# GpSimd scales by the reciprocal sum with "multiply, add zero" in place of "multiply"

## The reference

```python
x = x + ternary_linear(moe(x, cond))                 # layer 0: 8 experts, 2 chosen, 2 shared
c = attention(x)                                     # layer 1: 16 heads of 64, one null key
x = x + quantised_ffn(c)

def attention(x, attn_bias, mask, ...):
    xn = layernorm(x, g_in)
    q = heads(xn @ Wq) * scale; k, v = xn @ Wkv      # one key and value head for all 16 query heads
    sim = q @ k.T + attn_bias                        # (batch, 16, 512, 513 with the null key)
    sim = where(causal or not mask, -max, sim)
    attn = softmax(sim)
    return layernorm(attn @ v @ Wo, g_out)
```

## Time and profile before

| what | value |
|---|---|
| median of 3 runs | 1531.45 us (1531.21 to 1536.43) |
| the profiled execution: its time | 1530.96 us |
| the profiled execution: span of its instructions | 1528.9 us |
| busy PE / DVE / ACT / POOL | 1307.4 / 1059.4 / 762.5 / 870.0 us |
| instructions of POOL | 834, of which 512 are `normalise` (L837) |
| mean granted clock of TensorE | 0.933 of full speed |

### The profile page before, as it was taken

How to read it: one execution, slowest core, us unless ns; L and a number is a source line. 1 busy time by engine, 2 the same in 40 slices (tenths; PEclk the granted TensorE clock), 3 DMA queues, 4 the chain that set the end, 5 groups by cost and what they waited for, 6 DMA issues and landing times. The chain is left out here.

```text
span 1528.9 us, 30048 instructions
## 1 busy us (share of the span) xinstructions
PE 1307.4 (86%) x8710; PEld 1008.9 (66%) x8710; DVE 1059.4 (69%) x2788; ACT 762.5 (50%) x1940; POOL 870.0 (57%) x834
## 2 busy tenths in 40 slices
PE   4979999999934788999999999999999999963865
PEld 3868787778822566777777777777777777751222
DVE  5576666665564665887886777777878867862986
ACT  3313222223212444666665666666666666633853
POOL 1343332323323999778777777787787788930004
PEclk8999999999966788999999999999999999986987
DMA  6222210222026000001001000000000000202215
GB/s 219 101 81 98 97 65 32 96 83 74 10 76 220 15 1 1 1 2 30 2 2 31 1 24 7 2 29 3 2 29 2 2 16 1 72 1 59 69 42 178
DMA packets 51043, 71.55 MB, mean 47 GB/s; under 512 B 4497, under 2 KB 43665, under 8 KB 48850
## 3 DMA queue, kind: packets, MB, share of 16 engines
q1 hardware_dynamic: 50338, 69.60, 13.6%
q10 hardware_dynamic: 560, 0.20, 0.1%
HBM read 57.07 MB, written 12.72 MB: 46 GB/s over the span
## 5 line engine op out<-in xcount | busy, mean ns | idle before, releaser
L837 POOL TENSOR_SCALAR scores<-scores,att_rinv 128x128 f32<-128x128 f32 (+3 forms) x512 | 546.3, 1081 | 67.4 <-DVE att_rinv L1049 67.4
L893 ACT ACTIVATE scores<-scores,att_top 128x128 f32<-128x128 f32 (+3 forms) x512 | 282.9, 553 | 298.4 <-DVE att_top L1031 298.2
L1031 DVE CUSTOM_DVE_ANT_0 scores<-ps_y,w_bias_b,null_s 128x128 f32<-128x128 f32 x448 | 230.2, 548 | 131.9 <-PE ps_y L1181 118.7
L261 POOL TENSOR_TENSOR act_w<-act_g,wide_w 128x512 f32<-128x512 f32 x64 | 105.6, 1650 | 279.5 <-DVE act_g L379 273.9
L1180 PE MATMUL ps_y<-k_hh,q_hl 128*128 128x256 f32 (+2 forms) x512 | 191.0, 383 | 31.3 <-issue 17.8
L1192 PE MATMUL ps_up<-ident,scores 128*128 128x128 f32 x1280 | 192.5, 279 | 25.5 <-ACT keep L901 22.5
L1202 PE MATMUL ps_a<-keep,w_val 128*64 128x128 f32 x2560 | 201.6, 288 | 0.3 <-DVE keep L1059 0.3
L1192 PEld LDWEIGHTS ps_up<-ident,scores 128*128 128x128 f32 x1280 | 153.6, 142 | 51.8 <-issue 24.2
L208 ACT ACTIVATE hid_hi<-hid 128x512 fp32r<-128x512 f32 x80 | 50.5, 632 | 252.7 <-DVE hid L397 250.5
L1202 PEld LDWEIGHTS ps_a<-keep,w_val 128*64 128x64 f32 x2560 | 138.8, 139 | 42.7 <-issue 36.8
L1181 PE MATMUL ps_y<-w_k_lm,w_q_hm 128*128 128x256 f32 (+2 forms) x512 | 165.7, 333 | 0.0
(11 more groups left out here) (236 smaller groups left out, 2648.9 us busy)
## 6 DMA issues: line engine op xcount, KB each, us to landing
wide_w<-token_w_dram SPq DMA_DIRECT2D x16, 1024.0 KB, 4.7
x_raw<-in_x_t_dram SPq DMA_DIRECT2D x8, 512.0 KB, 3.8
x_nat<-in_x_nat_dram SPq DMA_DIRECT2D x8, 512.0 KB, 4.6
x_dram<-x_nat SPq DMA_DIRECT2D x8, 512.0 KB, 2.9
w_x1t<-x_dram SPq DMA_DIRECT2D x8, 512.0 KB, 4.0
c_dram<-out_raw SPq DMA_DIRECT2D x8, 512.0 KB, 3.3
c2t<-c_dram SPq DMA_DIRECT2D x8, 512.0 KB, 3.7
x_tile<-x_dram SPq DMA_DIRECT2D x8, 512.0 KB, 4.4
```

Source lines behind the costliest of these rows:

```text
L261: nc.gpsimd.tensor_tensor(act_w[:, k % 2], act_g[:, k % 2], wide_w[:, k], ALU.mult).then_inc(sem.act_w_ready, 1)
L837: nc.gpsimd.tensor_scalar(s, s, rinv[:, pp, q, hh:hh + 1], None, ALU.mult).then_inc(sem.p_normed, 1)
L893: nc.scalar.activation(s, s, ACT.Exp, scale=-1.0, bias=top[:, pp, q, hh:hh + 1], accum_out=lsum[:, pp, q, hh:hh + 1]).then_inc(sem.exp_don ...
L1031: dve.tensor_tensor_reduce(scores_of(pp, hh, q), psS[:, hh, 0:n], bias_of(w, h)[:, CAUSAL[q]:CAUSAL[q] + n], 1.0, null_s[:, par, q, h:h + ...
```

## The change

GpSimd's `tensor_scalar` in two places gets a second operation. The result is the same number (adding 0.0). No instruction is added, removed or moved on any engine: each engine's stream has the same rows in the same order as before. The first place runs 16 times (128 x 1280, the factor is the constant -1.0), the second 512 times (the four widths, the factor is a value for each partition read from `att_rinv`).

```diff
@@ def mask_diagonal(pool, nc, w, h, sem):
     pool.wait_ge(sem.bias_in[h], 16 * QB)
-    nc.gpsimd.tensor_scalar(bias_of(w, h), bias_of(w, h), -1.0, None, ALU.mult).then_inc(sem.bias_turned, 1)
+    nc.gpsimd.tensor_scalar(bias_of(w, h), bias_of(w, h), -1.0, 0.0, ALU.mult, ALU.add).then_inc(sem.bias_turned, 1)
     pool.wait_ge(sem.bias_turned, h + 1)
@@ def normalise(J, j):
                         s = scores_of(pp, hh, q)
-                        nc.gpsimd.tensor_scalar(s, s, rinv[:, pp, q, hh:hh + 1], None, ALU.mult
+                        nc.gpsimd.tensor_scalar(s, s, rinv[:, pp, q, hh:hh + 1], 0.0, ALU.mult, ALU.add
                                                 ).then_inc(sem.p_normed, 1)
```

## The result

The changed kernel takes 1494.6 us (median of 4, 1493.01 to 1495.32) beside 1532.72 us of the kernel before in the same runs: a ratio of 0.9744, 95% interval 0.9726 to 0.9763. The forecast was 1486 in a range of 1466 to 1504. The gain is 38 us, where the terms of the forecast add up to 45.

A forecast was written before the change was run, and what follows sets the result against it. TensorE was taken to bound the steady batches and GpSimd batch 0 while it has bias to turn. Terms of -25, -8, -6, -2 and -4 sum to -45 us on 1530.96: 1486 us, range 1466 to 1504.

The forecast's parts named there:

- Batch 0 is bound by GpSimd: Batch 0 from 522.9 us: TensorE becomes the bound, the stretch goes from 105.2 to about 80 us, -25 us.
- The 79.7 us that the steady pace gave: Batch 0 from 522.9 us: its 49 runs of L837 at the pace of 64 in a 104.1 us steady batch.
- The price: Multiply-add on GpSimd: 0.83 ns an element, 293 to 612 ns for the scores' four widths, 1250 ns for the bias.
- Start of batch 0: 482.8 to 522.9 us: 5 us back from VectorE's holds, 3 from earlier turns and quicker matmuls, -8 us.
- Steady batches: Six batches and the last: TensorE stays the bound, its idle time shrinks by 1 us a batch, -6 us.
- The mixture: Second batch, with the two early heads of bias: shorter VectorE holds leave about 1 us of the loss, -4 us.
- End of attention: Last eight score multiplications after the last reciprocal take 3.6 us instead of 8.50, -2 us.
- Rival 1: Scores and bias: only the constant-factor form is quick; 1501 us, chance 0.07.
- rival 2: L844, the query copy, is quick for its output type or narrower operand, not its operations; 1531 us, chance 0.09.
- Rival 3: Both GpSimd places: the second operation is paid; 1553 us at +20%, about 1655 at +50%, chance 0.06.

The follow-up runs named there:

- run 1: Kernel before with only the bias negation given the two-operation form, scores left at one operation; 1499.98 us, ratio 0.9769.
- run 2: Kernel before with only the scores' multiplication given the two-operation form, bias negation left at one operation; 1517.99 us, ratio 0.9875.
- run 7: Changed kernel with the scores' multiplication done on one column of each block only, so output is not the reference's; 1487.01 us, ratio 0.9699.
- run 6: Kernel before with each bias negation cut into four one-operation instructions of 128 x 320; 1538.56 us, ratio 1.0024.
- run 3: Changed kernel with the scores' multiplication back to one operation from batch 1 on; 1500.2 us, ratio 0.9757.
- after_again: The changed kernel unaltered, measured a second time beside two others on one chip; 1496.55 us, ratio to the kernel before 0.9767.
- run 4: Changed kernel with scores multiply-multiply (first head) and add-multiply (second), bias multiply-subtract, query copy a single multiplication; 1540.49 us, ratio 1.0033.

## Why the prediction was right, and where its sizes were off

- *Batch 0 is bound by GpSimd.* Right, and the bulk of the gain. Forecast -25 us, measured -28.7. The 79.7 us that the steady pace gave was too high. The stretch is six of the eight pairs, so 48 of L837 and not 49 are its share, which gives 77.9 us, and it has 558 matmuls where six eighths of 759 are 569, which gives 76.4; measured 76.5. Runs 1 and 2 show the cause: the same work on GpSimd, 14.5 us a pair, gives near the same stretch by two different ways.
- *The price.* Right for the rate in both forms, 0.84 ns. The fixed part with a per-partition factor was undersized by 85 ns a time, 44 us of GpSimd's busy time over 512. It was no term of its own in the sum, and run 7, which takes this part and more away, bounds what it can have cost.
- *Start of batch 0.* Forecast -8, measured -4.8. That VectorE's holds cost time is right (runs 1, 2 and 6). Their end was oversized. The layer norm's instructions of 128 x 4 did what was forecast: 7.7 us in that stretch before, 3.3 after. But I took one shorter instruction as the limit of a hold, and the larger L644 is now held for longer, 2464 ns where its longest was 767. TensorE waits 1.9 us for it (the third line of the changed kernel in run 6), 0.2 before. In the changed kernel's trace VectorE is held over two instructions in a row:

```profile
516.57 1.59 POOL L837 TENSOR_SCALAR scores<-scores,att_rinv 128x256 f32<-128x256 f32 x3
...
517.75 1.66 DVE L1039 TENSOR_TENSOR null_d<-att_top,null_s 128x8 f32<-128x8 f32 x1
...
518.14 1.25 POOL L601 TENSOR_SCALAR w_bias_b<-w_bias_b 128x1280 f32<-128x1280 f32 x1
```

  VectorE's small instruction starts under the last multiplication, and ends at 519.4 with the negation that follows. Its median in the whole kernel did fall, from 432 to 190 ns, its longest only from 2033 to 1655:

```profile
L1039 DVE TENSOR_TENSOR null_d<-att_top,null_s x64: 166/190/1655, 491.5 to 1304.5; 128x8 f32<-128x8 f32 x64
```

- *Steady batches.* Forecast -6, measured -1.2: the largest miss. The step that failed is that TensorE's 18.6 us of waits for ScalarE's copies come from VectorE's holds on L1039. The changed kernel has as many of them:

```profile
PE ps_up L1192 <- ACT keep L901: 19.4, 27, 1.0
```

  Over the six batches L1039 did fall, from 20.2 to 12.1 us, but the layer norm's instructions of 128 x 4 rose from 29.0 to 34.0, and VectorE as a whole is busy only 7 us less. Nor do these waits follow the scores' form: they are 18.4 to 18.8 us in the four kernels with the old form in these batches, 19.4 to 19.6 in the six with the new one. Only with 265 ns instructions (run 7), when VectorE is busy 24 us less than before, do some go:

```profile
PE ps_up L1192 <- ACT keep L901: 15.6, 22, 1.0
```

  The six batches then are 3.8 us shorter than in the changed kernel. So some 4 us of these waits go with GpSimd's work; what the rest comes from was not tested, and the order of ScalarE's own work is a guess. The 1.2 us, too, is read from one pair of profiles. The six batches take 628.3 to 631.5 us (mean 630.0) in the four profiles with the old form in them (the kernel before and runs 1, 3 and 6) and 626.3 to 628.2 (mean 627.1) in the six with multiply-add, and the last batch is 0.3 to 0.4 us longer with it. That makes some 2.5 us in place of the 6; 1.8 of them lie in the second and fourth batch, which vary most.
- *The mixture.* Forecast -4, measured -2.5 in the changed kernel's first profile. There the hold on the cast is gone (694 ns) and that on L352 fell from 2136 to 955 ns, but L384 and L355 are held too (1.73 and 1.06 us), and TensorE's wait of 4.47 us is still 4.86. In its second profile (`after_again`) the same stretch takes 13.8 us, the forecast. The start of the first negation and VectorE beside it, first profile and second:

```profile
82.28 1.27 POOL L601 TENSOR_SCALAR bias_a<-bias_a 128x1280 f32<-128x1280 f32 x1 [3.41 <-DMA bias_a<-in_bias_dram]
82.35 1.73 DVE L384 TENSOR_TENSOR hid_lo<-hid,hid_hi 128x512 fp32r<-128x512 f32 x1
```

```profile
83.15 1.26 POOL L601 TENSOR_SCALAR bias_a<-bias_a 128x1280 f32<-128x1280 f32 x1 [4.14 <-DMA bias_a<-in_bias_dram]
84.38 0.17 DVE L352 TENSOR_SCALAR amax<-amax 128x4 f32<-128x4 f32 x1
```

  GpSimd waits for the bias's transfer in both, and for longer where the stretch is shorter. So that wait by itself is not what costs; it decides when the negation starts, and with it which of VectorE's instructions are held. Of the six profiles with the quick negation in this place two have 15.6 us and four 13.7 to 14.1. The size of the term was right in most of them; what it missed is that it depends on the moment.
- *End of attention.* Forecast -2, measured 0. TensorE's turns and the copies between them set it, as the prediction feared; GpSimd was ahead of them in either form: its last multiplication ended at 1351.2 and TensorE began the last turns at 1352.1, and in the changed kernel at 1310.0 and 1315.3.
- *The rivals.* Rival 1 falls by L837's 699 ns, rival 2 by the query copy in run 4. Rival 3 is false for multiply-add but its mechanism exists: with subtract or maximum in the pair an element costs 0.8 ns more than the 2.5 of the multiplication alone. The Trainium skill's rule, "GPSIMD Engine Reference", section 3.1, that up to two operations for each element run at the rate of the port, is borne out by the quick forms (0.84 ns is 1.01 cycles at the page's 1.2 GHz) and not by the single multiplication (2.50 ns) or by multiply-subtract. I had it as a rule against the change; for `tensor_scalar` the pair of operations decides. A slip in the prediction: it has GpSimd idle for a third of its time after the change, where GpSimd is busy for 37% and idle for the rest.

## What to carry to other kernels

On GpSimd, write a float32 scaling as multiply then add 0.0 (or times 1.0): multiply alone cost three times as much for each element here, and a subtraction or maximum still more. Look for the gain in the stretch where GpSimd is the bound, however short: here 28.7 of 38 us came from one batch of eight, and in a steady batch 35 us less of GpSimd's time bought 0.2 to 0.5 us. Before counting on a wait that a faster engine shall shorten, check that the waited-for instruction was late because of it and not for another reason.

## What the runs showed that I had not expected

- GpSimd's `tensor_scalar` in float32 has three speeds by its operations. Multiply-add, multiply-multiply and add-multiply: 0.84 ns an element. Multiply alone: 2.50. Subtract-multiply and multiply-max: 3.34, and multiply-subtract about the same (4527 ns at the one width tried). Other pairs and types were not tried, and why the single form is slow is not known from these runs.
- A factor read for each partition adds about 85 ns to the quick form (128 x 512: 699 against 612 ns at 64 x 512 with constants, and 1260 ns at 128 x 1280 lies on the line of the constants).
- VectorE's hold by GpSimd can last over the following GpSimd instruction, when they run back to back (1.66 us for 128 x 8 elements, above). With the scores alone changed, an L644 took 4764 ns, though no instruction of GpSimd's there takes over 3.5 us. So a shorter instruction need not shorten a hold by its own saving.
